# Order of masking, weighing and adding heads in the mixing steps of a two-block transformer kernel

## The reference

```python
x = x + mlstm(layernorm(x), ctx, ctx, ...)      # the mixing
# inside, per head:
log_D = where(mask, cums[s] - cums[t], -inf) + ig[t]
D = exp(log_D - max_log_D)                      # decay tiles, causal
C = (q @ k.T / 8) * D                           # scores, weighed
normalizer = maximum(abs(C.sum(-1)), exp(-max_log_D))
h = (C / (normalizer + 1e-6)) @ v
hn = (h - mean) * rsqrt(var + 1e-6) * outnorm_weight
x = x + ffn(layernorm(x), w1, b1, w2, b2)       # the MLP
```

## Time and profile before

| | us |
|---|---|
| median of 3 runs | 1844.22 (1844.12 to 1845.14) |
| span of the profiled execution | 1843.2 |
| TensorE busy | 1663.1 (90%) |
| VectorE busy | 1209.8 (66%) |
| ScalarE busy | 843.8 (46%) |
| GpSimd busy | 608.1 (33%) |

### The profile page before, as it was taken

The page is one execution under the profiler, slowest core; times in us unless marked ns, Lnnn a source line. Parts: engine busy times, 40 slices in busy tenths (PEclk is TensorE's granted clock), DMA queues, the critical chain, the costliest instruction groups (busy, mean ns, idle before and its releaser), DMA issues. The chain is left out here.

```text
span 1843.2 us, 25796 instructions
## 1 busy us (share of the span) xinstructions
PE 1663.1 (90%) x8789; PEld 1128.1 (61%) x8789; DVE 1209.8 (66%) x2689; ACT 843.8 (46%) x1870; POOL 608.1 (33%) x730
## 2 busy tenths in 40 slices
PE   6569999996999999999999999999999999973584
PEld 4447777754666666666666666666666766642352
DVE  6445656532777777776776776776777677757761
ACT  3324343431555555555555555555555555531110
POOL 2143445430333323332332332333232323220375
PEclk9669999997999999999999999999999999985697
DMA  8100000003323232323232322222223223213254
GB/s 254 27 23 12 12 12 1 1 0 106 69 47 69 47 92 46 69 69 69 47 92 47 67 72 61 54 65 74 56 60 79 59 53 86 46 45 99 44 85 58
DMA packets 68961, 109.46 MB, mean 59 GB/s; under 512 B 18400, under 2 KB 50400, under 8 KB 68832
## 3 DMA queue, kind: packets, MB, share of 16 engines
q1 hardware_dynamic: 62688, 99.29, 22.1%
q0 software_dynamic: 6144, 8.52, 3.0%
HBM read 27.84 MB, written 12.85 MB: 22 GB/s over the span
## 5 line engine op out<-in xcount | busy, mean ns | idle before, releaser
L1128 POOL TENSOR_SCALAR at_Pr<-at_Pr,at_rinv 128x512 f32<-128x512 f32 x512 | 355.8, 695 | 841.2 <-DVE at_rinv L1158 841.2
L1093 ACT ACTIVATE at_Pr<-at_ps,at_nmax 128x512 f32<-128x512 f32 x512 | 352.2, 688 | 535.2 <-DVE at_nmax L1153 533.6
L1153 DVE TENSOR_REDUCE at_nmax<-at_ps 128x1 f32<-128x512 f32 x512 | 351.2, 686 | 154.0 <-PE at_ps L958 142.5
L958 PE MATMUL at_ps<-at_k,at_q 128*128 128x512 f32 x1024 | 420.7, 492 | 10.8 <-DMA at_k<-at_k_own 9.1
L969 PE MATMUL at_ps<-k_ident,at_Pr 128*128 128x128 f32 x2048 | 309.8, 274 | 4.5 <-POOL at_Pr L1128 4.5
L969 PEld LDWEIGHTS at_ps<-k_ident,at_Pr 128*128 128x128 f32 x2048 | 250.5, 140 | 90.2 <-POOL at_Pr L1128 27.7
L1165 DVE COPY at_PT<-at_ps 128x512 f32<-128x512 f32 x384 | 261.4, 681 | 0.0
L958 PEld LDWEIGHTS at_ps<-at_k,at_q 128*128 128x128 f32 x1024 | 174.6, 191 | 130.7 <-issue 121.2
L979 PE MATMUL at_ps<-at_PT,at_V 128*64 128x512 f32 x1024 | 235.4, 602 | 0.9 <-DVE at_PT L1165 0.9
L1158 DVE RECIPROCAL at_rinv<-at_rsum 128x1 f32<-128x1 f32 x512 | 83.3, 163 | 161.1 <-ACT at_Pr L1093 159.1
L979 PEld LDWEIGHTS at_ps<-at_PT,at_V 128*64 128x64 f32 x1024 | 68.1, 137 | 122.5 <-issue 121.4
(11 more groups left out here) (236 smaller groups left out, 1996.5 us busy)
## 6 DMA issues: line engine op xcount, KB each, us to landing
at_k<-at_k_own SPq DMA_DIRECT2D x256, 256.0 KB, 4.3
k_x<-in_x SPq DMA_DIRECT2D x8, 512.0 KB, 8.5
mg_ctx<-in_ctx SPq DMA_DIRECT2D x8, 512.0 KB, 8.7
mx_ctxn<-in_ctx SPq DMA_DIRECT2D x8, 512.0 KB, 3.8
rows<-m_ctxT SPq DMA_DIRECT2D x16, 256.0 KB, 2.6
out<-k_x SPq DMA_DIRECT2D x8, 512.0 KB, 3.5
r_w<-in_L_ffn_w SPq DMA_DIRECT2D x16, 256.0 KB, 5.5
mx_w<-in_L_ffn_w SPq DMA_DIRECT2D x2, 1024.0 KB, 10.0
```

The lines of the kernel that those rows point to most:

```text
L958: ins = pe.matmul(ps[:, S_BANK + j % 2, :], q2[:, u % 2, h, q:q + P], k2[:, u % 2, h, part, :], start=part == 0, stop=part == 1)
L1093: act.activation(Pr[:, j % 4, :], ps[:, S_BANK + j % 2, :], ACT.Exp, bias=nmax[:, j % 4:j % 4 + 1], accum_out=rsum[:, j % 4:j % 4 + 1]).th ...
L1128: pool.tensor_scalar(Pr[:, n % 4, :], Pr[:, n % 4, :], rinv[:, n % 4:n % 4 + 1], 1.0, ALU.mult, ALU.mult).then_inc(s["pn"], 1)
L1153: dve.tensor_reduce(nmax[:, j % 4:j % 4 + 1], ps[:, S_BANK + j % 2, :], AX.X, ALU.max, negate=True).then_inc(s["nmax"], 1)
```

## The change

GpSimd masks the first two decay tiles of batch m ahead of `add_heads(b+1)` instead of behind it. VectorE weighs the first two scores of batch m and then keeps the states of the first pair, both ahead of its wait for `xadd` and the statistics of batch b+1; before, the statistics came first, then the states, then the weighing. Norming follows the statistics directly. The instructions are the same.

```diff
@@ GpSimd, step(b) @@
                         norm_batch_pool(pool, s_out, b - 1, tmp_out, c["minus_half"])
-                    if there(b + 1):
-                        add_heads(b + 1)
                     if there(m):
                         mask(m, 0)
                         mask(m, 1)
                     if there(b + 1):
+                        add_heads(b + 1)
                         norm_batch_pool(pool, s_in, b + 1, tmp_in, c["minus_half"])
@@ VectorE, step(b) @@
                     if there(m):
                         scale_queries(m, 0)
+                    if there(m):
+                        weigh(m, 0)
+                        weigh(m, 1)
+                        keep_states(m, 0)
                     if there(b + 1):
                         dve.wait_ge(s["xadd"], b + 2)
                         norm_stats_dve(dve, s_in, b + 1, x_all, tmp_in)
-                    if there(m):
-                        keep_states(m, 0)
-                        weigh(m, 0)
-                        weigh(m, 1)
-                    if there(b + 1):
                         norm_apply_dve(dve, s_in, b + 1, x_all, tmp_in,
                                        lambda: wait_count(dve, s_in["turned"], b + 1))
```

## The result

The changed kernel takes 1851.78 us, the median of 6 runs (1849.93 to 1853.27), against 1844.68 us for the kernel before, measured beside it: a ratio of 1.0038 with a 95% interval of 1.0027 to 1.0048. It is slower by 7.1 us; forecast were 6.0. One of the six runs of the kernel before was in a slow state (8602.58 us); the ratio leaves it out, and without it the median before is 1844.22 us, the difference 7.6. The profiled execution spans 1851.3 us, 8.1 us more than the span before.

A forecast was written before the change was run, and what follows sets the result against it. TensorE, busy 39.58 of 40.36 us, was taken to set the full steps. Step -2 +0.3, step -1 -5.7 and six full steps +11.4 summed to +6.0 us: 1850.2 us, range 1845.0 to 1857.0.

The forecast's parts named there:

- Full steps: Six steps with MLP beside mixing (b = 0 to 5): each 1.9 us longer, 11.4 us in all.
- step -1: Step b = -1, without an MLP, where TensorE waits: `values(1, 0)` 5.7 us earlier, bounds 3.9 and 6.3.
- The chain of the full step: Heads, statistics, power, norming, queries in each full step: 2.0 us stall before `states(m, 1)`, 1.9 us delay at the end.
- TensorE's wait for `mm_qs`: Profile sign in full steps: TensorE waits 1.5 to 2.0 us for it before `states(m, 1)`.
- VectorE's wait for the add: Profile sign in full steps: VectorE idle about 4 us until GpSimd's add.
- Masks block the norming: Full steps: masks 2 and 3 lock out VectorE's norming, which takes 2.1 us, between 1.38 and 2.77.
- rival 1: Masks do not block the norming: each full step costs 1.2 us, time 1846.0 us; chance 0.14.
- The early stall at `values(m, 0)`: Full steps: TensorE waits about 0.5 us there, contained in the later 2.0 us stall.
- rival 3: First states fall behind the long add: step -1 gains 3.9 us, full steps lose 2.4 each, 1855.0 us; chance 0.12.
- The scaling of the heads beside a mask: VectorE in step -1: lengthened by the mask, ending at about 99.7 instead of 99.30.
- Step -2: Step b = -2, no heads to add; states behind the second weighing: +0.3 us, from 0 to +0.8.
- The clock: Rival: TensorE's clock falls in the full steps' new stalls, 8 to 17 us in five steps, 1859 to 1867; chance 0.12.

The follow-up runs named there:

- e1: Kernel before with the new order only in the steps without an MLP (b = -2 and -1): 1841.53 us, ratio 0.9979.
- e2: Kernel before with the new order only in the full steps (b = 0 to 5): 1855.45 us, ratio 1.0052.
- e3: Kernel before with VectorE's new order in all steps and GpSimd's old order: 1844.62 us, ratio 0.9995.
- e5: Changed kernel with masks 2 and 3 of batches 2 to 7 cut to 8 of 128 columns per tile: 1848.14 us, ratio 1.0014 to the kernel before.
- e4: As e1, with the long add of the heads of batch 0 cut into four adds of one tile: 1838.42 us, ratio 0.9964 to the kernel before.
- e7: The changed kernel run again unaltered, for a second profile: 1852.17 us (one run).
- e8: As e4, with GpSimd's add of a row for the outgoing batch moved ahead of mask 2: 1835.16 us, ratio 0.9942 to the kernel before.
- e6: Kernel before with GpSimd's new order in all steps and VectorE's old order: 1909.0 us (one run).

## Why the prediction was right, and where it was not

- *Full steps lose, step -1 gains, the loss wins.* Shown by e1 and e2, with opposite signs, and by the steps of 42.02 us.
- *The chain of the full step.* Forecast were queries 2.0 us late and `values(m, 1)` 1.9 us late. Counted from the start of `hidden`, `states(m, 1)` started at 32.75 us against 31.06 and `values(m, 1)` at 36.94 against 35.27: 1.7 us each. Two terms were too large: the norming took 1.92 instead of 2.1, and the heads 4.97 instead of 5.08 us. e3 shows that the GpSimd half of the change drives it, e5 that a term cut from it comes back in full. Two signs named for the profile were off: TensorE's wait for `mm_qs` was 0.82 us, not 1.5 to 2.0, as 0.7 of the 1.7 had been lost at `values(m, 0)` already, and VectorE's wait for the add was 2.20 us, not about 4; the forecast's own times (states to 270.8 or 271.5, add to 273.61) give 2.1 to 2.8.
- *Masks block the norming.* Taken over rival 1, and shown by e5: 0.54 us of norming, 0.52 per step.
- *The early stall at `values(m, 0)` is contained.* It was 0.46 us, about 0.5 forecast, and the stall before `states` ends when the queries come whatever lies ahead: the delay of the step, 1.66 us, is that of the queries, not a sum with it.
- *Step -1.* Here the forecast was off. It took 5.7 us and left the second chaining a slot before the long add; the profile has it behind the add, as rival 3 had it for this step, and e4 shows that cause. `values(1, 0)` started at 105.68 instead of 109.44, 3.8 us earlier against a bound of 3.9 for that case, and 3.2 us earlier counted from the start of the stage. It came 2.0 us after the 103.7 of the forecast: 1.47 is the long add (e4), 0.35 is that GpSimd's power ended at 98.38, not 98.03, and 0.16 stays when the add is cut (5.83 us behind the power, against 5.67 forecast). The 0.35 goes with the clock: `values(0, 1)` began 0.7 us earlier than before (86.40 against 87.11) but ran at the low level, and the next piece began 0.35 later (91.01 against 90.66), as the kernel before had the high level up to 88.4. The scaling of the heads beside a mask took 1.64 us, 0.4 more than alone, as forecast.
- *Step -2.* +0.3 forecast; `values(0, 0)` came 8.06 us after the start of the stage, not 7.84: +0.2.
- *The clock.* I had it as a rival in the full steps, where it stayed at 1.00. Where it counted was the start, where the sum had no term for it: of the 3.8 us at the end of step -1, 1.9 were gone at `hidden(0)`, as the kernel before had a high stretch there that the changed one had not. What sets where these stretches fall was not tested; e7 shows that they differ between two executions of one kernel.

So the total came out within 1.6 us with two errors that cancel in part: the full steps cost 10.1 us (5 x 1.66 + 1.78), not 11.4, and what precedes them brought 1.9, not 5.4, with 0.5 of the 1.9 from before the stage. That the total is so close is luck in part. The range held the time for the right main reason, not for the right size of the gain.

## What to carry to other kernels

An order that helps the one step with a hole can cost more in the steps without: price a reordering for each kind of step, and multiply. A long GpSimd instruction over SBUF is a place where a short VectorE instruction can be locked out, so look at what stands beside it; cutting it into pieces, or moving it beside work that has slack, gave 1.5 us in one step (e4) and 1.0 us in each of five (e8). If a wait on one engine is moved ahead of others' inputs, the whole queue behind it pays: here the same VectorE order was free with an early `xadd` (e3) and cost 1.66 us a step with a late one.

## What the runs showed of the hardware

- The lock-out goes both ways. In step -1 of the changed kernel the first mask began at 98.34 and the scaling of heads at 98.42; the scaling took 1.64 instead of 1.23 us, and the two masks with the scaling beside them took 2.21 instead of 1.27 us. So moving a mask of 0.64 us beside a VectorE operation cost both engines.
- GpSimd's power (L85, 1.02 us on 128x4) did not hold up the chaining of states in e6, though it reads SBUF: the pair ran beside it in 0.74 us, its time alone (e8's row). The Trainium skill ("SBUF — State Buffer", section "Who interferes with whom") has the lock held for the whole instruction; for the long adds and the masks the runs agree, for this instruction with few elements the measured time does not.
- With a stall of 7.19 us in a step otherwise dense, the clock was low for 10.2 us from within the stall on, in every full step (e6). With stalls of 0.46, 0.82 and 0.68 us in one step it stayed at 1.00 (the changed kernel).
